# Summing softmax weights over 16 heads: a tree of adds against a strided reduction on VectorE

## The reference, cut to what matters

```python
energy = jnp.einsum('bhqd,bhkd->bhqk', Qh, Kh) * scale
attn = jax.nn.softmax(energy, axis=1)
out = jnp.einsum('bhqk,bhkd->bhqd', attn, Vh)
out = out.transpose(0, 2, 1, 3).reshape(b, -1, D_MODEL)
return out @ Wo_w.T + Wo_b
```

## Time and profile before

| what | value |
|---|---|
| median of 3 runs | 2376.84 us (2374.91 to 2378.2) |
| time of the profiled execution | 2374.91 us |
| span of the profiled execution | 2373.1 us |
| TensorE busy (matmuls) | 1875.3 us, 79% of the span |
| VectorE busy | 1171.4 us, 49% |
| ScalarE busy | 811.2 us, 34% |
| mean granted TensorE clock | 0.89 of full speed |

### The profile page before, as it was taken

One profiled execution on the slowest core, in us unless ns is written; L12 is line 12 of the kernel. 1 busy time (PEld: TensorE's weight loads), 2 busy tenths in 40 slices (PEclk: granted clock), 3 DMA queues, 4 the chain that ended last, 5 costly groups with the idle time before them and its releaser, 6 DMA issues.

```text
span 2373.1 us, 31423 instructions
## 1 busy us (share of the span) xinstructions
PE 1875.3 (79%) x10791; PEld 1327.4 (56%) x10792; DVE 1171.4 (49%) x2229; ACT 811.2 (34%) x1752; POOL 242.8 (10%) x234
## 2 busy tenths in 40 slices
PE   2799998369476876447899889999986775499998
PEld 2456555257354553333454447778764443399997
DVE  2434342550688888774454343543456664522221
ACT  2243423022243342232343343221237774132221
POOL 1010100043200000002010000000010000133332
PEclk9999998579687887767999999999998897599999
DMA  8442422412722412023432240000035552442221
GB/s 270 58 63 32 58 28 71 165 29 37 135 36 35 58 27 28 5 50 50 60 52 39 28 198 2 2 2 1 2 65 71 73 68 93 170 138 35 36 38 29
DMA packets 91645, 144.42 MB, mean 61 GB/s; under 512 B 13509, under 2 KB 80589, under 8 KB 88141
## 3 DMA queue, kind: packets, MB, share of 16 engines
q1 hardware_dynamic: 76156, 115.38, 22.4%
q0 software_dynamic: 15360, 27.28, 7.2%
HBM read 75.63 MB, written 27.79 MB: 44 GB/s over the span
## 4 chain that ended last, share of the span: by engine, by line
PE 60%; DVE 15%; DMA 10%; issue 6%; SPq 4%; ACT 4%; DVEq 0%; POOL 0%; ACTq 0%; POOLq 0%
PE ps L822 10%; PE ps L1141 10%; PE ps L1216 6%; PE ps L1227 6%; DMA Qpack<-QP 3%; PE ps L1126 3%; PE ps L785 3%; PE ps L866 3%; PE ps L813 3%; DMA Kpack<-pad_rows 2%; SPq L458 2%; PE ps L1051 2%; PE ps L1061 2%; ACT pT L1343 2%; DMA bq<-in_bq 2%
## 5 line engine op out<-in xcount | busy, mean ns | idle before, releaser
L822 PE MATMUL ps<-pT,V 128*32 128x256 f32 x1536 | 295.4, 402 | 41.5 <-DVE V L1759 41.5
L1740 DVE TENSOR_REDUCE mx<-ps 128x2 f32<-128x512 f32 x256 | 165.4, 686 | 170.7 <-PE ps L788 93.0
L1338 ACT ACTIVATE pT<-ps 128x512 f32<-128x512 f32 x256 | 150.5, 597 | 246.3 <-PE ps L816 139.9
L813 PE MATMUL ps<-Qpack,Kpack 99*128 99x256 bf16 (+1 forms) x768 | 167.3, 288 | 41.2 <-ACT pT L1343 17.3
L822 PEld LDWEIGHTS ps<-pT,V 128*32 128x32 f32 x1536 | 104.0, 112 | 162.8 <-issue 62.1
L1216 PEld LDWEIGHTS ps<-xgT,XNT 128*128 128x128 f32 x1280 | 150.5, 194 | 1.9
L1216 PE MATMUL ps<-xgT,XNT 128*128 128x128 f32 x1280 | 150.6, 276 | 0.0
L1227 PE MATMUL ps<-w,mid 128*128 x640 | 144.6, 379 | 0.0
L785 PE MATMUL ps<-Kpack,Qpack 97*128 97x256 bf16 x512 | 109.1, 289 | 42.4 <-DMA Kpack<-pad_rows 22.5
L813 PEld LDWEIGHTS ps<-Qpack,Kpack 99*128 99x128 bf16 (+1 forms) x768 | 70.3, 101 | 121.9 <-ACT pT L1338 42.9
L1343 ACT ACTIVATE pT<-ps,nmax 128x256 f32<-128x256 f32 x256 | 118.3, 498 | 56.1 <-DVE nmax L1750 55.5
(11 more groups left out here) (303 smaller groups left out, 3378.0 us busy)
## 6 DMA issues: line engine op xcount, KB each, us to landing
Qpack<-QP SPq DMA_DIRECT2D x192, 128.0 KB, 6.9
w<-in_w SPq DMA_DIRECT2D x16, 1024.0 KB, 6.6
Kpack<-KP POOLq DMA_DIRECT2D x96, 128.0 KB, 5.4
Kpack<-KP SPq DMA_DIRECT2D x96, 128.0 KB, 4.2
ctxT<-in_ctxT SPq DMA_DIRECT2D x32, 256.0 KB, 6.2
h<-h_rows SPq DMA_DIRECT2D x2, 4096.0 KB, 22.1
wd<-in_wd SPq DMA_DIRECT2D x4, 1536.0 KB, 15.1
xn_rows<-xn SPq DMA_DIRECT2D x16, 256.0 KB, 2.8
```

Of the source, the lines that this page charges most:

```text
L813: mm = pe.matmul(A[h % ring][:, t], Kpack[par][0:rows, h, t * P:(t + 1) * P], Qpack[par][0:rows, h], start=True, stop=L != 0)
L822: mm = pe.matmul(O[c // 2][r0:r0 + VW, c % 2], V[par][:, t, h], weights[:, t], start=t == 0, stop=t == ST - 1)
L1338: act.activation(pT[h % 4][:], A[h % 2][:], ACT.Exp).then_inc(s["exp_done"], 1)
L1740: dve.tensor_reduce(mx[:, :, h], A[2 + h % 2][:], AX.X, ALU.max).then_inc(s["smax_done"], 1)
```

## The change

`sums1` sums over the heads in another way, and `hpart` becomes smaller.

- Before, for each key tile: two adds of 4 heads to 4 heads (1,024 elements a partition each, each after half of the exponentials), an add of the two results (1,024), an add of 512, an add of 256, then the reciprocal.
- After, for key tile 0: two reductions, each over 8 heads (2,048 elements read, 256 written, each after half of the exponentials), an add of 256, then the reciprocal.
- After, for key tile 1: one reduction over all 16 heads (4,096 elements read, 256 written), after all 16 groups of exponentials of the item, then the reciprocal.
- The reductions read `probs` in the order "query, then head", so that two reads in a row are 1 KB apart. The multiplication at the end is as before.
- The steps that pass through the semaphore `sum1_step` go from 12 to 6 for each batch item.

```diff
-        hpart = sb("hpart", [P, 2, GROUP, S], F32, att)
+        hpart = sb("hpart", [P, 2, S], F32, att)
...
                 def sums1(b, t):
 
-                    base = 12 * b + 6 * t
-
-                    def step(k, e):
-                        e.then_inc(s["sum1_step"], 1)
-                        dve.wait_ge(s["sum1_step"], base + k)
-
-                    for half in range(2):
-                        first, second = half * HPH, half * HPH + GROUP
-                        dve.wait_ge(s["exp1_done"], 16 * b + 8 * t + GROUP * (half + 1))
-                        e = dve.tensor_tensor(hpart[:, half], probs[:, t, first:first + GROUP], probs[:, t, second:second + GROUP], ALU.add)
-                    e.then_inc(s["sum1_step"], 2)
-                    dve.wait_ge(s["sum1_step"], base + 2)
-                    step(3, dve.tensor_tensor(hpart[:, 0], hpart[:, 0], hpart[:, 1], ALU.add))
-                    step(4, dve.tensor_tensor(hpart[:, 0, 0:2], hpart[:, 0, 0:2], hpart[:, 0, 2:4], ALU.add))
-                    step(5, dve.tensor_tensor(hsum[:, t], hpart[:, 0, 0], hpart[:, 0, 1], ALU.add))
-                    step(6, dve.reciprocal(hsum[:, t], hsum[:, t]))
+                    steps = 4 if t == 0 else 2
+                    base = 6 * b + 4 * t
+                    if t == 0:
+
+                        for half in range(2):
+                            hh = slice(half * HPH, (half + 1) * HPH)
+                            dve.wait_ge(s["exp1_done"], 16 * b + 4 * (half + 1))
+                            dve.tensor_reduce(hpart[:, half], probs[:, t, hh].rearrange("p h q -> p q h"), AX.X, ALU.add).then_inc(s["sum1_step"], 1)
+                        dve.wait_ge(s["sum1_step"], base + 2)
+                        dve.tensor_tensor(hsum[:, t], hpart[:, 0], hpart[:, 1], ALU.add).then_inc(s["sum1_step"], 1)
+                    else:
+                        dve.wait_ge(s["exp1_done"], 16 * (b + 1))
+                        dve.tensor_reduce(hsum[:, t], probs[:, t].rearrange("p h q -> p q h"), AX.X, ALU.add).then_inc(s["sum1_step"], 1)
+                    dve.wait_ge(s["sum1_step"], base + steps - 1)
+                    dve.reciprocal(hsum[:, t], hsum[:, t]).then_inc(s["sum1_step"], 1)
+                    dve.wait_ge(s["sum1_step"], base + steps)
                     dve.tensor_tensor(probs[:, t], probs[:, t], hsum[:, t].unsqueeze(1).to_broadcast([P, H, S]), ALU.mult)\
                         .then_inc(s["norm1"], 1)
```

## The result

The changed kernel takes 2405.81 us (median of 4 runs, 2402.26 to 2408.95), the kernel before 2377.52 us (median of 4 runs). The ratio is 1.0119, with a 95% interval of 1.0099 to 1.014: some 28 us slower, where 10 us faster was forecast.

The account below looks back on a forecast made before the run. VectorE's sums were taken to bound each attention 1 slot. Savings of 0.93 us (key tile 0) and 0.37 us (key tile 1), 1.30 us in 8 items, gave 10.4 us: 2366.4 us from 2376.84, range 2359 to 2378.

Parts of the forecast that it names:

- What bounds the kernel: Attention 1: each slot is one loop through VectorE's sums, so a microsecond off the sums is one off the slot.
- the forecast slot: Attention 1, from the first add of one slot to that of the next: about 43.0 us in place of 44.3.
- The price of an element, 1.042 ns: VectorE's f32 reductions in `sums1`: 1.042 ns for each further element, from multiplication and add lengths; upper end 2.08 ns.
- The sum's terms 2.29 and 4.43 us: Forecast lengths of the `sums1` reductions: 2.29 us for 2,048 elements (key tile 0), 4.43 us for 4,096 (key tile 1).
- 1.30 us saved: Forecast gain in `sums1` for each batch item: 0.93 us in key tile 0 plus 0.37 us in key tile 1.
- the break-even of 1.25 ns: Element price in the `sums1` reductions at which the 1.30 us gain is used up, 20% above 1.04 ns.
- The rows it rested on: Four trace rows of near forms (two-place, 16 strided elements, 16-deep strided reduction), taken to show strided reads cost almost nothing more.
- The first half's longer reduction hides in the wait for ScalarE.: Key tile 0: the first reduction, 2.29 for 1.23 us, ends at 831.67, 0.43 us before the eighth group is there.
- Cover for the wait for all 16 groups: Key tile 1: the single reduction's wait for all exponentials costs nothing, with 4.3 us of cover.
- slack of `rest_k` and TensorE: After the sums: `rest_k` keeps 0.86 us to spare; TensorE's idle time before `values1` shrinks from 4.40 to about 3.1 us.
- The clock rival: TensorE after its idle time: shorter idling keeps the clock at 2.4 GHz, 16 us more gain, 2351 us; chance 0.03.
- The strided reads are dear: Rival, an item's three `sums1` reductions: at a doubled element price 6.81 us an item lost, 54 us, 2431 us; chance 0.14.

## Why the prediction was wrong

- **What bounds the kernel.** Right. The slot is one loop through VectorE's sums: each key tile's part came out at the device time (16 and 11 us, 27 together), and the forecast lengths gave the forecast slot (43.16 us) once the reads were in order.
- **The price of an element, 1.042 ns, "the value I take".** This step failed. The reductions cost (7,065 - 157) / 4,096 = 1.69 ns an element, with the 157 ns of fixed time of the prediction's own working. The sum's terms 2.29 and 4.43 us were therefore 3.72 and 7.07 us, and 1.30 us saved became 3.68 us lost in each item. The 1.69 ns are over the break-even of 1.25 ns which the rival had given, and under the 2.08 ns taken as its upper end.
- **The rows it rested on.** The numbers were read rightly, and each was taken for more than it shows. The two-place reduction, 693 ns, is free because it has two places: four places cost in full. The row of the 16-deep strided reduction, 557 ns, reads PSUM, where 1 KB apart is free as well (4,424 ns); from SBUF, 16 deep and 32 bytes apart cost 7,466 ns. The rows of 16 strided elements, 178 and 179 ns, are too short: with 16 elements the extra shows as 4 ns, with 256 as 158. The prediction subtracted them as if every element counted alike.
- **"The first half's longer reduction hides in the wait for ScalarE."** This held with reads in order (the second reduction still waited 0.38 us). At 3.7 us it does not hide: the two run back to back in 7.32 us. This overlap failed with the price and not by itself.
- **Cover for the wait for all 16 groups; slack of `rest_k` and TensorE.** Right: neither key tile 1's reduction nor `rest_k` waited for ScalarE, in the changed kernel or in the one that reads in order, and TensorE kept idle time before `values1` in both (8.09 and 2.81 us).
- **The clock rival.** It did not come about. In the changed kernel, after the longer idle time, the granted clock is 0.50 from 882 to 886 us and 0.85 from 886 to 890. With reads in order, after 2.81 us of idle time, it is still 0.50 from 852.4 to 856 us, 0.70 from 856 to 860, and 1.00 only after that.
- **The rival.** *The strided reads are dear* was the right mechanism, with the right place and break-even, at a chance of 0.14; its 54 us were for a doubled price, and the price rose by 0.65 ns, not 1.04. Its end was left out of the range. The Trainium skill's rule (Advanced Engine Details and Errata, section SBUF Cachelines) named this cost: a different 16-byte line on each access brings a penalty, and two hits on a line absorb it. The runs agree with it in most forms: 8 bytes apart is free (two reads in a line) and 16 is not, and runs of two floats are free. They do not agree where two places are read in turn: each read goes to another line, and yet 512 elements take 692 ns, where 512 contiguous ones took 681. The prediction had set it aside on rows of 16 elements.

## What to carry to other kernels

On f32 in SBUF, a VectorE reduction or add whose reads land 16 bytes or more apart each time, and that goes round four places or more, cost about 1.7 ns an element and not 1.04; a tree of adds over contiguous heads does fewer elements (3,840 for 4,096) at the low price. Laying the data out for the reduction did not help here, because the engines that write and read it then had to scatter single floats. Whether they would be spared by runs of two floats, as VectorE's adds are, was not tried. Before a price is taken from a row, check that the row has the same memory, the same number of places and enough elements for the cost to show above the instruction's start.

## What the runs showed of the hardware

- Reading single f32 from scattered places in SBUF costs extra on more than one engine: 4,096 of them take 7.13 us in a VectorE add and 7.12 us in a ScalarE copy, though contiguous they take 4.43 and 3.62 us. Scattered writes cost as much (ScalarE, 7.13 us). Reads of PSUM 1 KB apart cost nothing extra on either (4,424 and 3,584 ns).
- The sum is not the same for every instruction: VectorE's copy goes from 2.29 to 4.60 us. Why it stays below the others was not tried.
- It does not depend much on the distance: 16 bytes 7.32 us, 32 bytes 7.47, 64 bytes 6.98, 1,024 bytes 7.00, 1,028 bytes 7.43.
- Three places in turn are almost free (1,032 ns for 768 elements), four cost in full (1,885 ns for 1,024). Why the step lies there, and why the first elements of an instruction are free, was not tried.
- TensorE pays for its moving data too: eight matmuls of 256 columns with the weights 64 bytes apart took 1.90 us in place of 1.06, both at a granted clock of 1.00.
